# The product of up and gate weights in two halves, in a fused Flamingo-like block on one core

## The reference, cut to what matters

```python
u = jnp.einsum('nh,ehi->eni', xt, Wup) + bup[:, None, :]
g = jax.nn.silu(jnp.einsum('eni,eij->enj', u, Wgate) + bgate[:, None, :]) * u
eo = jnp.einsum('enj,ejh->enh', g, Wdown) + bdown[:, None, :]
```

## Time and profile before

| what | us |
|---|---|
| median of 3 runs (1070.67 to 1079.22) | 1074.09 |
| the profiled execution, own time | 1068.86 |
| its span in the profile | 1067.0 |
| PE busy | 832.3 (78%) |
| PE weight loads | 518.2 (49%) |
| DVE busy | 595.7 (56%) |
| ACT busy | 431.3 (40%) |
| POOL busy | 321.8 (30%) |

### The profile page before, as it was taken

One profiled execution on the slowest core, in us unless ns is written; L12 is line 12 of the kernel. 1 busy time (PEld: TensorE's weight loads), 2 busy tenths in 40 slices (PEclk: granted clock), 3 DMA queues, 4 the chain that ended last, 5 costly groups with the idle time before them and its releaser, 6 DMA issues. The chain is left out here.

```text
span 1067.0 us, 16839 instructions
## 1 busy us (share of the span) xinstructions
PE 832.3 (78%) x4613; PEld 518.2 (49%) x4626; DVE 595.7 (56%) x1409; ACT 431.3 (40%) x954; POOL 321.8 (30%) x535
## 2 busy tenths in 40 slices
PE   0699996766657798887189967799997946999990
PEld 0455552333323355575058854456666623666660
DVE  8589985888847666665013237688885602111114
ACT  0456662555413312232016753466663211333330
POOL 2000022233256622114703773200020271133331
PEclk9999999555569986658689997999997887999995
DMA  9200012100040057542313535100000021122217
GB/s 328 76 22 21 21 62 98 56 0 0 0 131 1 10 226 226 155 158 94 124 50 91 156 112 184 42 22 19 19 3 1 31 104 54 45 67 87 77 46 236
DMA packets 65790, 86.91 MB, mean 81 GB/s; under 512 B 11517, under 2 KB 58288, under 8 KB 64570
## 3 DMA queue, kind: packets, MB, share of 16 engines
q1 hardware_dynamic: 58954, 69.18, 20.7%
q0 software_dynamic: 6768, 16.86, 4.5%
HBM read 48.47 MB, written 35.01 MB: 78 GB/s over the span
## 5 line engine op out<-in xcount | busy, mean ns | idle before, releaser
L1464 DVE TENSOR_TENSOR ctx_cols<-ctx_cols,ps 128x256 f32<-128x256 f32 x54 | 22.7, 421 | 140.1 <-ACT ctx_cols L950 119.1
L740 ACT ACTIVATE probs_t<-ps 128x1024 f32<-128x1024 f32 x64 | 65.6, 1024 | 72.4 <-PE ps L1594 72.4
L1087 DVE TENSOR_REDUCE row_max<-ps 128x8 f32<-128x1024 f32 x64 | 77.8, 1216 | 5.1 <-PE ps L1584 2.6
L1093 DVE TENSOR_TENSOR work<-ps,row_max 128x1024 f32<-128x1024 f32 x64 | 77.7, 1214 | 3.4
L573 POOL COPY work<-ctx_rows 128x256 f32 (+1 forms) x32 | 12.7, 400 | 216.2 <-PE ps L1605 216.2
L1975 PE MATMUL ps<-early,xt 128*128 x152 | 71.4, 592 | 0.5
L550 POOL DMA_INDIRECT y_rows<-ctx_cols,w2d x38 | 37.3, 981 | 110.1 <-ACT ctx_cols L962 96.5
L734 ACT ACTIVATE work<-work 128x1024 f32<-128x1024 f32 x64 | 67.3, 1051 | 8.0 <-DVE work L1093 8.0
L1594 PE MATMUL ps<-ident,work 128*128 128x128 f32 x512 | 69.1, 278 | 1.4 <-ACT work L734 1.4
L950 ACT ACTIVATE ctx_cols<-ps 128x256 f32<-128x256 f32 x54 | 20.7, 384 | 115.4 <-PE ps L1975 82.1
L1594 PEld LDWEIGHTS ps<-ident,work 128*128 128x128 f32 x512 | 55.9, 141 | 15.3 <-ACT work L734 10.1
(11 more groups left out here) (335 smaller groups left out, 1967.3 us busy)
## 6 DMA issues: line engine op xcount, KB each, us to landing
work<-x_rows SPq DMA_DIRECT2D x77, 129.0 KB, 2.1
x_rows<-wgb SPq DMA_DIRECT2D x1, 5031.0 KB, 19.5
x_rows<-wgb SPq DMA_DIRECT2D x1, 4902.0 KB, 35.0
early<-in_w3st SPq DMA_DIRECT2D x8, 512.0 KB, 4.9
work<-y_rows SPq DMA_DIRECT2D x16, 256.0 KB, 3.1
early<-y_rows SPq DMA_DIRECT2D x8, 512.0 KB, 7.3
late<-in_w2u SPq DMA_DIRECT2D x1, 2304.0 KB, 8.2
x<-in_x SPq DMA_DIRECT2D x4, 512.0 KB, 5.2
```

The lines of the kernel that those rows point to most:

```text
L740: act.activation(probs_t[:, :, :], ps[:, 4:6, :], ACT.Copy).then_inc(sem("att.evac"), 1)
L1087: dve.tensor_reduce(row_max[:, u, 8 * c:8 * c + 8], scores(c), AX.X, ALU.max).then_inc(sem("att.max"), 1)
L1093: dve.tensor_tensor(probs[:, u, c, :].rearrange("p (h k) -> p h k", k=P), scores(c), row_max[:, u, 8 * c:8 * c + 8].unsqueeze(2).to_broadc ...
```

## The change

`fuse(0)` to `fuse(3)` stay in iterations 4 to 7. `fuse(4)` to `fuse(7)` follow the whole loop on PE, each with a bank of its own (0 to 3), so without a wait on ACT between them; `fuse(4)` waits until ACT and DVE are done with those banks. The bias sum in bank 7 is made in two groups of four, and DVE adds it in two steps (at i = 10, and behind the first `take_back2`). ACT copies four products in its iterations 5 to 8 and four behind the loop. PE's first slot tile waits for four copies, not eight. POOL's first two pairs of deviations come ahead of the split of `brow`, not behind it, and the split waits for both additions. SP issues the six later `back2` ahead of `wd3` and the bias parts, not behind them.

```diff
+        EARLY = 4
+        def fuse_bank(e):
+            return 6 if e < EARLY else e - EARLY
...
             back2(0)
             back2(1)
+            for q in range(2, NT // 2):
+                sp.wait_ge(sem("resid5"), 2 * q - 2)
+                back2(q)
             upto(sp, "wp.mm", E3 + 1)
             sp.dma_start(wd3, a["w3dn"]).then_inc(sem("load.w3f"), 16)
             sp.wait_ge(sem("bias.part"), 8)
             sp.dma_start(b24[8:16, :], bmid).then_inc(sem("b3.rows"), 16)
             sp.wait_ge(sem("bias.part"), 10)
             sp.dma_start(b24[16:24, :], blo).then_inc(sem("b3.rows"), 16)
-            for q in range(2, NT // 2):
-                sp.wait_ge(sem("resid5"), 2 * q - 2)
-                back2(q)
             stage_attention(sp, 3)
...
             send_back(2, N2, xd2, y2, y_rows2, dest2)
-            pool.wait_ge(sem("b3.row"), 1)
+            dev6 = deviation(6)
+            dev6(0, True, False)
+            dev6(2, False, False)
+            pool.wait_ge(sem("b3.row"), 2)
             pool.tensor_copy(b24[0:E3 + 1, :], brow).then_inc(sem("bias.part"), 1)
...
-            dev6 = deviation(6)
-            dev6(0, True, False)
-            dev6(2, False, False)
             for t in range(0, NT, 2):
...
+            def product_out(e):
+                upto(act, "wp.mm", e + 1)
+                act.activation(w13[:, e, :, D:2 * D], bank(fuse_bank(e)).rearrange("p (j n) -> p j n", j=2), ACT.Copy
+                               ).then_inc(sem("wp.out"), 1)
...
-                if 5 <= i < 6 + E3:
-                    e = i - 5
-                    upto(act, "wp.mm", e + 1)
-                    act.activation(w13[:, e, :, D:2 * D], bank(6).rearrange("p (j n) -> p j n", j=2), ACT.Copy
-                                   ).then_inc(sem("wp.out"), 1)
+                if 5 <= i < 5 + EARLY:
+                    product_out(i - 5)
...
+            for e in range(EARLY, E3 + 1):
+                product_out(e)
...
+            def add_rows(n):
+                upto(dve, "wp.mm", n)
+                dve.tensor_tensor(brow[:, D:2 * D], ps[0:E3 + 1, 7, 0:D], brow[:, D:2 * D], ALU.add).then_inc(sem("b3.row"), 1)
...
-                if i == 14:
+                if i == 10:
                     dve.wait_ge(sem("load.brow"), 32)
-                    upto(dve, "wp.mm", E3 + 1)
                     seq(dve.memset(b24, 0.0))
-                    dve.tensor_tensor(brow[:, D:2 * D], ps[0:E3 + 1, 7, 0:D], brow[:, D:2 * D], ALU.add).then_inc(sem("b3.row"), 1)
+                    add_rows(EARLY)
...
             take_back2(0)
+            dve.wait_ge(sem("b3.row"), 1)
+            add_rows(E3 + 1)
             norm_x(6, 0)
             take_back2(2)
...
                 if e == 0:
                     upto(pe, "rt2.read", 1)
-                else:
+                elif e < EARLY:
                     upto(pe, "wp.out", e)
+                elif e == EARLY:
+                    upto(pe, "s2.x", N2)
+                    upto(pe, "m2.h", NT + N2)
+                    upto(pe, "m2.ht", NT + N2)
...
                     if i + 1 == NT:
-                        upto(pe, "wp.out", E3 + 1)
+                        upto(pe, "wp.out", EARLY)
...
-                if 4 <= i < 5 + E3:
+                if 4 <= i < 4 + EARLY:
                     fuse(i - 4)
+            for e in range(EARLY, E3 + 1):
+                fuse(e)
+            upto(pe, "wp.out", E3 + 1)
+            pe.wait_ge(sem("b3.row"), 2)
```

More of the change, by code:

```diff
@@ L1850, in fuse @@
                     upto(pe, "rt2.read", 1)
-                else:
+                elif e < EARLY:
                     upto(pe, "wp.out", e)
+                elif e == EARLY:
+                    upto(pe, "s2.x", N2)
+                    upto(pe, "m2.h", NT + N2)
+                    upto(pe, "m2.ht", NT + N2)
                 up_t, ga = wst[:, e % 4, 0], wst[:, e % 4, 1]
                 for j in range(2):
-                    mm(ps[0:E3 + 1, 7, 0:D], bupz[:, e, j, :], ga[:, j, :], start=(e == 0 and j == 0),
-                       stop=(e == E3 and j == 1), skip_group_check=True)
+                    mm(ps[0:E3 + 1, 7, 0:D], bupz[:, e, j, :], ga[:, j, :], start=(e in (0, EARLY) and j == 0),
+                       stop=(e in (EARLY - 1, E3) and j == 1), skip_group_check=True)
                 for c in range(2):
                     for j in range(2):
-                        op = mm(ps[:, 6, c * D:(c + 1) * D], up_t[:, j, c * P:(c + 1) * P], ga[:, j, :], start=(j == 0),
+                        op = mm(ps[:, fuse_bank(e), c * D:(c + 1) * D], up_t[:, j, c * P:(c + 1) * P], ga[:, j, :], start=(j == 0),
                                 stop=(j == 1))
```

## The result

The changed kernel takes 1063.8 us (median of 10 runs, 1061.39 to 1068.65) beside 1074.44 us for the kernel before (10 runs, 1069.46 to 1079.69). The ratio is 0.9904, with a 95% interval of 0.9876 to 0.9931: 10.3 us faster (7.4 to 13.3 by the interval). Forecast were 1062.0 us, 12.1 us less, in a range of 1054 to 1069.

A forecast was written before the change was run, and what follows sets the result against it. PE was taken to bound the shared and slot tiles and to wait behind them. Profiled 1068.86 - 14.1 + 0 + 2.0 + 0 = 1056.8 us; from the median, 1074.09 - 12.1 = 1062.0 us, range 1054 to 1069.

The forecast's parts named there:

- What bounds the stages: From 545 to 645 us: PE bounds shared and slot tiles, then waits 13.4 us for results.
- First half: Shared tiles: without four of the `fuse` products the first slot tile comes 14.1 us earlier; bounds 0 and 14.1.
- the rival: First slot tile: slot rows may set it, capping the gain at about 7.7 us, 1066.4 us in all; chance 0.27.
- Second half: Behind the slot tiles: four late products, 11.2 us, fit into PE's 13.4 us wait; cost 0, at worst 11.2.
- The gain bound: First queries: a PE gap of 2.2 us would keep the high clock, worth 1 to 2 us; counted as 0.
- POOL's split: Queries' stretch: split moved behind two deviations delays the third pair; cost 2 us, bounds 0 and 6.35.
- SP's queue: SP's list: `wd3`, bias parts and key staging come later, still in time for attention; cost 0, up to 5 us.
- The sum: Whole kernel: 12.1 us less than the median of 1074.09, giving 1062.0 us, 1.1% less.
- the capped gain: Either slot rows set the first slot tile or POOL's split costs its whole 6.35 us: 1066.4 us; chance 0.27.
- Late signals: Behind POOL's last sends of results: the signal of `fuse(7)` delayed by 12 to 21 us, up to 1080 us; chance 0.06.
- Missed cover: Behind the slot tiles: products stretched to twice 11.2 us outlast PE's wait by 9 us, 1071 us; chance 0.07.

The follow-up runs named there:

- e12: Changed kernel with POOL's second sixteen sends of rows in layer 2 held until PE has turned shared tile 8: 1057.73 us, one time.
- e1: Changed kernel with POOL's split behind the loop of the queries and its two DMAs among the key staging: 1050.4 us, ratio 0.9824 to the kernel before.
- e2: Changed kernel with most of the late products left out, 20 of 48 matmul records of experts 4 to 7 kept: 1053.8 us, one time.
- e4: Changed kernel with POOL's list as before, the split ahead of the first two pairs of deviations: 1060.8 us, one time.
- e10: Changed kernel once more, no edit, on another chip: 1065.43 us, ratio 0.989 to the kernel before.
- e6: Changed kernel with three products early and five late, expert 7's weights loaded behind the first loads of results: 1060.06 us, ratio 0.9909.
- e8: Changed kernel with two products early, six late, and POOL's split behind the loop of the queries: 1058.38 us, ratio 0.989.
- e11: Repeat of e1 next to e10, no new edit: 1060.13 us, ratio 0.983 to the kernel before.
- e3: Changed kernel with SP's list as before, wd3 and the bias parts ahead of the six later loads of results: 1064.2 us, one time.

## Why the prediction was right

**What bounds the stages.** Right. PE sets the shared and the slot tiles, and it waits behind them.

**First half, 14.1 us.** Right in both pairs of profiles: 14.0 and 14.7. The slot rows were there 5.8 us early, as worked out (5.4). I had this margin as the weak point of the forecast, with "each us by which the wait is more than 5.4 us shorter is lost". In these pairs it was not: SP issues the slot loads right behind the fourth product (540.91 in the earlier trace rows, 546.67 after), so the rows move with the wait and the margin stays. e12 shows the case that the rival meant: with the long wait gone PE is idle 17.52 us for the rows, and the first slot row follows the last send's end by 4.3 us.

Whether all executions gain the whole 14.1 no profile shows. In e1, e2 and e4, whose code is the same up to here, the fourth product got through at 525.9 to 527.8, while POOL was still sending, and a further wait came behind it. In e1 (1873 is the product, 1902 a turn, 1887 a turned slot row):

```profile
525.91 1.86 PE L1873 MATMUL ps<-early,mid 128*8 128x256 f32 x4 [14.68 <-ACT early L877]
...
539.07 0.48 PE L1902 MATMUL ps<-ident,xn 128*128 128x128 f32 x1 [6.17 <-DVE xn L1399]
...
548.75 0.38 PE L1887 MATMUL ps<-ident,work 128*128 128x128 f32 x2
```

The first slot row comes 22.3 to 22.8 us behind the fourth product in these three, and still 5.7 to 7.2 us earlier than in the first profile. In such an execution the kernel before might get a further product through in the meantime, which would take its 3.5 us out of the sum; neither of its two profiles is of this kind, so that is argued only.

**Second half, 0.** Right: 13.06 and 13.90 us beside 13.38 and 13.40, and e2 shows that taking most of the products away leaves this passage as it was. The 13.90 of e10 are not the products' doing: DVE did not wait for them there, but 3.82 us (2.99 in the first profile) ahead of its first addition of returned results. The cover was closer than stated: DVE's addition ended 0.34 us before the deviations came, where I had about 0.7, since four products took 11.6 us and not 11.2. That this addition takes less than 0.5 us was right (0.41), though its 256 columns are half of those of line 1433 and not a quarter. e6 and e8 show the edge: five late products cost 2.5 us, six 5.8.

**The gain bound, PE's clock.** I held that a gap of some 2 us would keep the high clock for the first queries. In the changed kernel it did for 2 us only. The gap was 1.53 us, the clock stayed at its high level until 638 and then fell to 1.2 GHz all the same (0.63 in the stretch 638 to 639, then 0.50 until 648), with PE busy 1.54 of the 1.80 us before. I had put no gain on it, so the sum did not suffer. In e1 the gap was 1.42 us, the clock was 1.00 over the first 3.2 us, and the queries took 1.3 us less than before; so a gain of the size that I named seems to be there once the split is out of the way, in executions in which the clock stays up; nothing isolates it.

**POOL's split, +2.0.** The size was right: +2.13 in both pairs, -2.1 in e4, and e1 and e11 get back 3.5 and 2.4. The path was not. I had POOL's own list as what delays the third pair, and DVE's held-up additions as something that ends before POOL's root mean square and so costs nothing. They did end before it, but behind them stand DVE's statistics of the third pair, for which POOL's deviations wait. They start 0.30 us after the last step of the statistics has begun, in both kernels (648.10 after 647.80; before, 654.56 in the earlier trace rows after this row):

```profile
654.26 0.17 DVE L976 COPY mv<-mv 128x4 f32<-128x4 f32 x1
```

POOL was idle for 0.39 us at that point in both profiles of the changed kernel, so its own end would have given at most 0.4 us less, some 1.7 us. By the rows of DVE the three operations took 3.7 us longer than before (1.86, 0.63 and 1.25), of which 1.34 replace a wait for ACT that DVE had there before; that is the 2.1 us within 0.3. So the forecast of 2.0 came out because the two paths end within 0.4 us of each other, which is luck. The rule of the Trainium skill reaches further than I used it: "SBUF — State Buffer", section "Who interferes with whom", names `tensor_scalar` among the operations that can enter a mode with two ports, and says that this mode contends with GpSimd. The trace agrees with a hold-up of that kind, though it doesn't show the mode: the normalization of the second pair, a `tensor_scalar`, took 2.59 us and not 0.73, and 0.74 in e1 without the split beside it. The additions took 1.31 and 1.94 us and not 0.69.

**SP's queue, 0.** Right, and e3 shows what the move prevents, 7.3 us.

**The sum.** 12.1 us forecast, 10.3 to 11.9 measured (the two ratios). The forecast lies inside the first interval (7.4 to 13.3 us), so no shortfall is shown in the times. More than 1% faster had the best chance, 0.60; the measured 0.96% falls under "within 1%", which had 0.34, and the interval holds both. In the profiles a term is missing, the attention, which I took to move as a block: it was 2.3 and 0.9 us longer. In the first pair 1.3 us lie ahead of its last scores, with PE at a granted clock of 0.76 from 684 to 688 (1.00 before), and 1.0 behind, with 0.54 over its last 5.8 us (0.86 before). Whether that comes from the change or from the moment is open: the other profiles of changed kernels have 127.0 to 128.9 us there, the two of before 126.9 and 127.0.

**The rivals.** Late signals behind POOL's last sends did not occur: DVE waited 0.49 us for the last product. Missed cover did not occur either. Of the capped gain, neither form occurred in the two pairs; e12 shows the first.

## What to carry to other kernels

Work that fills an engine in a stage which it bounds belongs where that engine waits, but only as much as the wait covers: here 11.6 us fit into 13.1 and a fifth product did not. Each consumer of the moved work has its own list, and what stands in it behind the new wait moves too; POOL's and SP's lists would have cost 4.7 and 7.3 us if left, and another place for POOL's split (behind the queries) gave another 2.4 to 3.5. An engine's own list is not the whole path: the split cost its 2.1 us through the DVE operations that ran beside it. If an early part of an execution has a wait whose length is chance, compare stage by stage, since the spans of a single pair of profiles showed 3.7 us where ten runs show 10.3.

## What the runs showed of the hardware

- While POOL issues indirect DMAs back to back, 1.27 us apart, signals from PE reached the other engines late. In the changed kernel PE's projection ended at 516.56 and ACT began its silu at 538.30, 21.7 us later and 3.1 us after the last send's end:

```profile
515.53 1.03 PE L1893 MATMUL ps<-late,xt_all 128*128 128x256 f32 x4
```

```profile
538.30 0.28 ACT L893 ACTIVATE xn<-ps 128x128 f32<-128x128 f32 x1 [27.34 <-remote]
```

  In the kernel before, DVE began an addition at 536.83 for which PE had been done since 509.85. The wait doesn't always last as long as the sends: in e1 ACT went on at 521.51 and waited again until 538.42, with the last send over at 534.07. A pause of 9 us after sixteen sends (e12, one execution) took the long wait away, and the kernel with the pause was among the fastest. In slot tiles, with one send in 1.6 us and other work between, there is no such delay. In the kernel before no packet of the instruction queues moved between 489 and 553, so the waits there are not for instructions being loaded. The cause behind it was not isolated.
- A normalization on DVE, with inputs and output in SBUF, took 2.59 us and not 0.73 beside POOL's operations on eight partitions.
- The granted clock of PE fell to its low level some 2 us after the end of a gap of 1.53 us, with PE busy 1.54 us of the first 1.80 behind the gap. Behind gaps of 1.42 and 1.39 us (e1, e12) it was 1.00 over the first 3.2 and 4.2 us.
